# Index lists loaded per round into a doubled buffer, and comparisons on one row of 640, in a two-layer graph network

## What is computed

```python
# layer 0
h = x @ W
e = leaky_relu((h @ att_src)[src] + (h @ att_dst)[dst], 0.2)   # loops (i, i) added to the edges
e = exp(e - segment_max(e, dst)[dst])
alpha = e / (segment_sum(e, dst)[dst] + 1e-16)
x = layernorm(x + tanh(segment_sum(h[src] * alpha[:, None], dst) + bias))
# layer 1
h = gelu(x @ W_pre + b_pre)
x2 = x + segment_sum(h[src] * edge_attr, dst)
y = gelu(gelu(x2 @ W1 + b1) @ W2 + b2)
out = layernorm(x + x2 + y)
```

## Time and profile before

| | |
|---|---|
| median of 3 runs | 3725.67 us (3724.6 to 3725.97) |
| span of the profiled execution | 3722.8 us |
| busy: PE, DVE, ACT, POOL | 2393.6, 2438.3, 1283.2, 2781.1 us |
| gathers L690 | 2850, 946 ns each |
| PE's granted clock | 0.50 in most of layer 0, about 0.94 in layer 1 |

### The profile page before, as it was taken

The page is one execution under the profiler, slowest core; times in us unless marked ns, Lnnn a source line. Parts: engine busy times, 40 slices in busy tenths (PEclk is TensorE's granted clock), DMA queues, the critical chain, the costliest instruction groups (busy, mean ns, idle before and its releaser), DMA issues.

```text
span 3722.8 us, 66966 instructions
## 1 busy us (share of the span) xinstructions
PE 2393.6 (64%) x16704; PEld 1951.7 (52%) x16705; DVE 2438.3 (65%) x6240; ACT 1283.2 (34%) x3893; POOL 2781.1 (75%) x2950
## 2 busy tenths in 40 slices
PE   6433343434344444444445988989888989999888
PEld 3333333333333333333334777777776777777776
DVE  7444444444466666566666777777777788888886
ACT  5433343434445555555553111111111221111222
POOL 7777777777777777777775777777777777777776
PEclk7555555555555555555557999999999999999998
DMA  5222221222222222222223343443334343444332
GB/s 102 43 42 42 41 44 42 44 42 43 42 43 44 43 44 43 43 44 45 44 45 99 93 94 90 95 94 94 95 91 96 93 96 91 97 95 99 93 95 70
DMA packets 351632, 254.26 MB, mean 68 GB/s; under 512 B 254125, under 2 KB 279218, under 8 KB 351387
## 3 DMA queue, kind: packets, MB, share of 16 engines
q0 software_dynamic: 94016, 146.16, 17.8%
q1 hardware_dynamic: 242753, 99.71, 11.7%
q10 hardware_dynamic: 14618, 6.14, 0.6%
HBM read 244.43 MB, written 7.25 MB: 68 GB/s over the span
## 4 chain that ended last, share of the span: by engine, by line
POOL 60%; issue 24%; ACT 4%; DVE 4%; PE 3%; DMA 2%; ACTq 1%; DVEq 1%; POOLq 0%; SPq 0%
POOL rows L690 60%; ACT onehot L747 1%; DMA rows<-table,src_i 1%; DMA src_i<-in_src_dram 1%; PE bank L1086 1%; ACT L790 1%; ACTq L740 0%; ACT pair L767 0%; DVE score L1361 0%; PE bank L1029 0%; PE bank L962 0%; ACT rowu L796 0%; DVE bst L1399 0%; ACT unused L790 0%; DVE newp L1352 0%
## 5 line engine op out<-in xcount | busy, mean ns | idle before, releaser
L690 POOL DMA_INDIRECT rows<-table,src_i x2850 | 2694.8, 946 | 896.0 <-issue 859.5
L1086 PE MATMUL bank<-node,hot 128*128 128x288 bf16 x9310 | 1228.4, 294 | 28.1 <-issue 16.5
L995 PE MATMUL bank<-onehot,rows 128*97 128x72 f32 (+1 forms) x3048 | 584.9, 369 | 814.9 <-ACT onehot L777 814.9
L1086 PEld LDWEIGHTS bank<-node,hot 128*128 128x128 bf16 x9310 | 932.2, 101 | 282.4 <-issue 20.9
L995 PEld LDWEIGHTS bank<-onehot,rows 128*97 128x97 f32 x3048 | 530.8, 281 | 854.4 <-issue 792.5
L1505 DVE TENSOR_SCALAR hot<-node,key 128x642 bf16<-128x642 int16 x1862 | 870.3, 539 | 130.8 <-PE bank L1086 80.0
L900 ACT ACTIVATE pair<-dst_i 128x8 f32<-128x8 int32 x196 | 35.2, 180 | 1175.3 <-DVE rows L1531 904.3
L747 ACT ACTIVATE onehot<-iota,far_dst 128x72 f32 (+1 forms) x1564 | 384.4, 328 | 23.0
L1339 DVE SCALAR_TENSOR_TENSOR other<-onehot,bank 128x576 f32<-128x576 f32 (+1 forms) x196 | 121.9, 622 | 404.1 <-ACT bank L760 335.4
L1073 PE MATMUL bank<-onehot,rows 128*96 128x40 f32 (+1 forms) x3128 | 306.8, 256 | 88.4 <-DVE rows L1536 50.6
L1073 PEld LDWEIGHTS bank<-onehot,rows 128*96 128x96 f32 x3128 | 295.8, 170 | 110.1 <-issue 88.7
(11 more groups left out here) (204 smaller groups left out, 1931.1 us busy)
## 6 DMA issues: line engine op xcount, KB each, us to landing
attr<-in_edge_attr_dram SPq DMA_DIRECT2D x190, 336.0 KB
rows<-table,src_i POOLq DMA_INDIRECT x2850
node<-in_src_dram SPq DMA_DIRECT2D x195, 64.0 KB
attr<-in_edge_attr_dram SPq DMA_DIRECT2D x190, 48.0 KB
dst_i<-in_dst_dram SPq DMA_DIRECT2D x200, 4.0 KB
src_i<-in_src_dram SPq DMA_DIRECT2D x195, 4.0 KB
src_i<-in_src_dram SPq DMA_DIRECT2D x190, 3.5 KB
dst_i<-in_dst_dram SPq DMA_DIRECT2D x190, 3.5 KB
```

Source lines behind the costliest of these rows:

```text
L690: pool.indirect_dma_start(rows[:, u, j * width:(j + 1) * width], None, table, bass.IndirectOffsetOnAxis(ap=src_i[:, u, j:j + 1], axis=0))\
L995: last = pe.matmul(total[:, 0:w], rows0(u, it)[:, j, 0:D1], wide(weights, w)[:, j, :], start=j == 0, stop=j == most - 1)
L1086: last = pe.matmul(p_got[t], hot[:, c % HOTS, i, t * P:(t + 1) * P], tab[:, a, :, :].rearrange("p k d -> p (k d)"), start=a == 0, stop=a = ...
```

## The change

Index lists: `src_i` and `dst_i` get a leading dimension of 2, `src_next` goes. SP loads a whole round's lists with one transfer each into the half that the round does not use (`round_of`, `load_round1`), so a round's five groups share `e.src[0]` and `e.dst[0]`. In layer 0 it does that when the round before the running one is fully released; in layer 1 after the `attr` loads of slot 4 of each round. POOL waits once a round for the list and, from round 2 of layer 0 and round 1 of layer 1 on, at each slot for `free >= 5 it + u + 1` itself. `rounds` writes two rounds in a loop's body. `load_booked_src` becomes one transfer. ACT and DVE find the round's half of `dst_i` by a computed address (`dst_here`). The last group's lists are loaded one group earlier.

Comparisons: `src16` is one row of 640, `hot` is written as one row of 640 (of 642 in memory).

```diff
-        src_i = sb("src_i", [P, SLOTS, TILES], INT32)
+        src_i = sb("src_i", [P, 2, SLOTS, TILES], INT32)
-        src_next = sb("src_next", [P, SLOTS, TILES], INT32)
-        dst_i = sb("dst_i", [P, SLOTS, TILES], INT32)
+        dst_i = sb("dst_i", [P, 2, SLOTS, TILES], INT32)
...
-        src16 = node[:, at_src16:at_got].bitcast(INT16).rearrange("p (r e) -> p r e", r=3)
+        src16 = node[:, at_src16:at_got].bitcast(INT16)[:, 0:BOOKED * P]
...
+        def rounds(eng, body, alone):
+            for it in range(alone):
+                body(it, it % 2)
+            with eng.Fori(alone // 2, (ROUNDS - 1) // 2) as pair:
+                for k in range(2):
+                    body(pair * 2 + k, k)
+            body(ROUNDS - 1, (ROUNDS - 1) % 2)
...
+            def round_of(to, of, it, k, landed, ahead=0):
+                sp.dma_start(to[:, k, :, :], of_round(of, it, ahead).rearrange("u (p j) -> p u j", j=TILES))\
+                    .then_inc(landed, 16)
...
+            def load0(it, k):
+                if not first(it):
+                    sp.wait_ge(e0.free, (it + 1) * SLOTS)
+                if it is ROUNDS - 1:
+                    return
+                if first(it):
+                    sp.wait_ge(e0.dst[0], 16)
+                round_of(dst_i, dst, it, 1 - k, e0.dst[0], 1)
+                if not first(it):
+                    round_of(src_i, src, it, 1 - k, e0.src[0], 1)
...
+            def load1(it, k):
+                for u in range(SLOTS):
+                    load_attr(it * SLOTS + u, it, u)
+                    if u == 0 and not first(it):
+                        load_booked_src(it)
...
+                if it is not ROUNDS - 1:
+                    load_round1(it, k)
...
-                    pool.wait_ge(e.src[u], 16 * (it + 1))
-                    pool.sem_inc(g_go, 1)
...
+            def gather1(it, k):
+                pool.wait_ge(e1.src[0], 16 * (it + 1))
+                pool.sem_inc(g_go, 1)
+                for u in range(SLOTS):
+                    if not first(it):
+                        pool.wait_ge(e1.free, it * SLOTS + u + 1)
+                        pool.sem_inc(g_go, 1)
+                    for j in range(TILES - booked(it, u)):
+                        row_gather(rows[:, u, j * D:(j + 1) * D], table1, src_i[:, k, u, j:j + 1], e1.rows[u])
...
-                act.activation(src16[:, :, 0:ROW3], src_all.rearrange("p (r e) -> p r e", r=3), ACT.Copy)\
-                    .then_inc(g_src16, 1)
+                act.activation(src16, src_all[:, 0:BOOKED * P], ACT.Copy).then_inc(g_src16, 1)
...
-                    last = v.tensor_scalar(hot[:, c % HOTS, i, :].rearrange("p (r e) -> p r e", r=3),
-                                           src16[:, :, 0:ROW3], key[:, a:a + 1], None, ALU.is_equal)
+                    last = v.tensor_scalar(hot[:, c % HOTS, i, 0:BOOKED * P], src16, key[:, a:a + 1], None, ALU.is_equal)
```

More of the change, by code:

```diff
@@ L523, in _ @@
             sp.dma_start(x1[0:LAST_N, (CHUNKS - 1) * CB, 0:D], x[(CHUNKS - 1) * CN:N, :]).then_inc(s_x[-1], 16)
[L524 to L530, removed]
+            round_of(dst_i, dst, 0, 0, e0.dst[0])
+            sp.wait_ge(e0.src[0], 16)
+            round_of(src_i, src, 1, 1, e0.src[0])
             sp.dma_start(w_prex[0:D, :], w_pre).then_inc(s_w, 16)
@@ L550, in store_table @@
                 sp.dma_start(table0[(CHUNKS - 1) * CN:N, :], x1[0:LAST_N, (CHUNKS - 1) * CB, :]).then_inc(a_st, 16)
[L552 to L564, removed]
-                    sp.dma_start(dst_i[0:m, u, 0:t], dst[bass.ds(g * GE, n)].rearrange("(p j) -> p j", j=t))\
-                        .then_inc(e.dst[u], 16)
-                    if attrs:
-                        sp.dma_start(attr[0:m, u, 0:t * D],
-                                     edge_attr[bass.ds(g * GE, n), :].rearrange("(p j) d -> p (j d)", j=t))\
-                            .then_inc(e.attr[u], 16)
-                return body
@@ L637, in _ @@
             store_table()
[L638 removed]
+            rounds(sp, load0, alone=2)
+            load_last(e0)
             sp.wait_ge(e0.free, GROUPS + SLOTS)
[L640 removed]
+            round_of(src_i, src, 0, 0, e1.src[0])
+            round_of(dst_i, dst, 0, 0, e1.dst[0])
+            rounds(sp, load1, alone=2)
+            sp.wait_ge(e1.free, LAST + 1)
+            load_last(e1)
+            sp.dma_start(attr[0:LAST_E // LAST_T, 0, 0:LAST_T * D],
+                         edge_attr[LAST * GE:E, :].rearrange("(p j) d -> p (j d)", j=LAST_T)).then_inc(e1.attr[0], 16)
             sp.wait_ge(f_o, MCHUNKS + 1)
@@ new lines, in gather_last, with gather0 @@
+            def gather_last(e, free, table, width):
+                pool.wait_ge(s_last, 16)
+                pool.wait_ge(free, LAST + 1)
+                for j in range(LAST_T):
+                    row_gather(rows[:, 0, j * width:(j + 1) * width], table, src_last[:, j:j + 1], e.rows[0])
+            def gather0(it, k):
+                for u in range(SLOTS):
+                    if first(it):
+                        pool.wait_ge(e0.src[u], 16)
+                        for j in range(TILES):
+                            row_gather(rows0(u, it)[:, j, 0:D], x, src_i[:, 0, u, j:j + 1], e0.rows[u])
+                        continue
+                    if u == 0:
+                        pool.wait_ge(e0.src[0], 16 * (it + 1))
+                        pool.sem_inc(g_go, 1)
+                    if second(it):
+                        if u == 0:
@@ L689, in body @@
-                    for j in range(TILES - (e is e1 and booked(it, u))):
-                        pool.indirect_dma_start(rows[:, u, j * width:(j + 1) * width], None, table,
-                                                bass.IndirectOffsetOnAxis(ap=src_i[:, u, j:j + 1], axis=0))\
-                            .then_inc(e.rows[u], 16)
-                return body
-            groups(pool, gather(e0, table0, D2), alone=2)
+                        pool.wait_ge(e0.rows[u], 16 * TILES)
+                    else:
+                        pool.wait_ge(e0.free, it * SLOTS + u + 1)
+                        pool.sem_inc(g_go, 1)
@@ L696, in _ @@
+            rounds(pool, gather0, alone=2)
+            gather_last(e0, e0.free, table0, D2)
             pool.wait_ge(m_st, STORED)
-            groups(pool, gather(e1, table1, D), alone=1)
+            rounds(pool, gather1, alone=2)
+            gather_last(e1, e1.free, table1, D)
         @block.scalar
```

128 lines of the change are left out of this document (65 added, 63 removed).

## The result

The changed kernel takes 3736.88 us, median of 8 runs (3734.95 to 3738.14), against 3725.84 for the kernel before (8 runs, 3724.44 to 3728.23). The ratio is 1.0029 [1.0020, 1.0038], 11.0 us slower. The forecast was 22 us slower. The direction was right, and so was the rule for what a single gather loses. The one term that carried the forecast is half of what was expected, because gathers don't come at any phase to the comparisons.

The account below looks back on a forecast made before the run. POOL, issuing gathers without a break, was taken to bound the kernel. Span 3722.8 + 0 for loads, addresses and DVE's saving + 22 for held gathers = 3744.8; the runs' median is 2.9 above that span, so 3748; range 3724 to 3790.

Parts of the forecast that it names:

- The loads, gain 0: Index loads per round and POOL's own slot wait: POOL has no wait for a load to win, so 0.
- Computed addresses off POOL's path, 0: ACT's and DVE's computed addresses for dst lie off POOL's path and cost 0.
- The comparison at 370 ns: Layer 1's comparison on one row of 640 runs at a quarter of the plain rate, 370 ns against 539.
- DVE's saving is worth 0: Faster comparisons take 313 us of DVE work off layer 1, worth 0 because DVE is not last there.
- A gather loses T - 0.125 - x above an onset: A gather starting x after a DVE operation of length T loses this, for x above an onset of 0.075.
- Gathers come every 1.249 us, at any phase: Averaging the loss over all phases in layer 1: 0.0116 us per comparison, times 1862 = 22 us.
- rival B: A gather needs the shared way twice, for its indices and its writing: twice 22, 3770; chance 0.12.
- A: One-row comparison keeps its pace, two a step, and leaves gathers alone: 3726; chance 0.13.
- C: Comparison keeps its 0.539 but holds gathers back as the copy L1423 does: 86 us, 3811; chance 0.05.
- E: The round's index list lands late, at 20 us costing 230: 3956; chance 0.02.
- F: New order frees POOL's wait at slot starts, at the full gap 390 x 0.30 = 117 faster: 3609; chance 0.03.
- D: DVE doesn't let POOL in between two comparisons of a run: 400 us, 4126; chance 0.04.

Follow-up runs that it names:

- the kernel with the larger operation: Changed kernel with an unused reduction over 2 x 80 numbers before each comparison: 3753.86 us, ratio 1.0080.
- The widths 752 and 512: Changed kernel with each comparison 752 numbers wide, 3758.76 us; with each 512 wide, the fifth slot's comparisons left out, 3732.95 us.
- two experiments: Changed kernel with comparisons reading 32-bit numbers, 3871.23 us; changed kernel with an unused reduction of 2 x 16 numbers before each comparison, 3787.45 us.

## Why the prediction was right and wrong, step by step

**What bounds the kernel: right.** POOL issues without a break, and the time followed the gathers' lengths.

**The loads, gain 0: right.** With them alone the kernel is at 1.0005 [0.9996, 1.0014], and POOL has no wait for `src_i` behind the first.

**Computed addresses off POOL's path, 0: slightly wrong.** ACT's first operation of each group waits longer, beginning with the kernel before (busy, mean ns, idle before), then the changed one:

```profile
L744 ACT ACTIVATE far_dst<-dst_i 128x8 f32<-128x8 int32 x196 | 40.8, 208 | 147.0 <-issue 147.0
```

```profile
L793 ACT ACTIVATE far_dst<-dst_i 128x8 f32 (+1 forms) x196 | 40.8, 208 | 168.0 <-issue 147.4 <-DMA dst_i<-in_dst_dram 20.7
```

21 us more over 196 groups, 0.107 each. Between the layers POOL waits for layer 0's last groups, which are worked off one after the other; the distance of two of these went from 7.46 to 7.52 us in the median, and POOL's wait from 27.7 to 28.7. In the kernel with the loads alone the same group shows 168.1 and the wait 28.6; with the comparisons alone they are 147.3 and 27.7. So the 1.0 us belongs to the half of the change with the loads and the addresses.

Which of the two it is can be seen within one trace. ACT computes the address only in the groups of its loops; in the rounds that are written out the address is a constant, while the list comes in one piece in both. Nothing else in ACT's part of layer 0 was changed but the semaphore that it waits for. The timelines of ACT, the kernel before and then the changed one (a shape of `dst_i` is printed only where the address is a constant):

```profile
919.69 0.21 ACT L744 ACTIVATE far_dst<-dst_i 128x8 f32<-128x8 int32 x1 [0.84 <-issue]
929.14 0.21 ACT L744 ACTIVATE far_dst<-dst_i 128x8 f32<-128x8 int32 x1 [0.69 <-issue]
```

```profile
919.48 0.21 ACT L793 ACTIVATE far_dst<-dst_i 128x8 f32 x1 [0.93 <-issue]
929.27 0.21 ACT L793 ACTIVATE far_dst<-dst_i 128x8 f32<-128x8 int32 x1 [0.69 <-issue]
```

In the 175 groups with a computed address the idle time is 0.120 us longer than before, in the 21 with a constant one 0.001 (with the loads alone 0.120 and 0.007). So the computed address makes the 21 us; the 20.7 that the page puts down to the load of `dst_i` are the idle times of 23 groups in which that load was the last event, and most of each is there before the change too. That POOL's 1.0 us comes from these 0.12 a group was argued from the distances, not tested by itself.

**The comparison at 370 ns: right.** The source view of the changed kernel, ns min/median/max:

```profile
L1554 DVE TENSOR_SCALAR hot<-node,key x1862: 366/379/629, 2011.4 to 3681.0; 128x640 bf16<-128x640 int16 x187
```

Undisturbed it takes 366. The mean of 399 contains what gathers take from it, which is why DVE saved 251 us and not 313. The table of modes of the Trainium skill ("VectorE: DVE Perf Modes", § The perf-mode tier table) gives four numbers a step for this form; the trace agrees, since 512, 640 and 752 numbers take 332, 366 and 395 ns at least, 0.26 ns a number, a quarter of the 1.05 of the earlier trace rows.

**DVE's saving is worth 0: right**, and the kernel with the larger operation shows the other end of it.

**A gather loses T - 0.125 - x above an onset: right for a gather's start.** An x of 0.10 costs 0.156, 0.15 costs 0.106; the onset lies at 0.085, where I had taken 0.075 (at 0.08 to 0.10 some pay and some don't). It is not the whole cost of such operations: the second access above has no term in the sum, and in this kernel it needs none.

**"Gathers come every 1.249 us, at any phase": this step failed.** It turned the rule into 0.0116 us for each of 1862 comparisons. Length and onset aren't to blame: with the measured 0.38 and 0.085 in the same formula T - 0.125 - a stays 0.170, and the sum stays 22. Spread evenly, 1862 x 0.02/1.249 = 30 gathers would start in each 0.02 us behind a comparison's start. There are at most 17 from 0.08 to 0.22, and 355 from 0.22 to 0.24, where the loss is 0.007. The term of 22 us measures 10.1 by single gathers and 11.45 by the stretch. The hint stood in the rows that I had used against rival B: the scaling's own lengths of 310 to 552 show DVE held by gathers in mid-gather. I asked whether this costs POOL a second time, and didn't ask where it puts DVE's next operation. Today's three-row comparisons, which nothing holds, are indeed at any phase (the kernel with the loads alone), and I had carried this over to comparisons that are held. The widths 752 and 512 moved the locked phase to 0.20 to 0.22 (gathers lose 31.0 us) and to 0 and 0.27 (4.7 us): the lock is shown by these, not argued.

**The rivals.** A, C and E didn't come. F, a faster start of the slot, didn't either: the gap is 0.30 at any gather. B and D were given chances of 0.12 and 0.04 and don't show in this kernel, but two experiments show that what they were made of is real: a gather needs the shared way a second time, and it can then get it only at the end of a comparison, sometimes of the last of the run. I had discarded D on one gather that got on between two operations; it got in at its start, and the second access is another matter.

The SBUF page of the Trainium skill ("SBUF — State Buffer", § Who interferes with whom) says that a two-port operation of DVE and one of GpSimd exclude each other for the whole instruction. For DVE's operations the trace agrees in the main: a gather that starts more than 0.085 after one waits until 0.125 before its end. For the gather it doesn't: comparisons start and run at full pace beside most of its 0.94 us (0.37 at 2060.25, 0.28 into a gather). Those that start 0.50 to 0.70 after it are held as a rule (medians of 0.45 to 0.56), many of those at 0.70 to 0.80 too (0.39 and 0.45), and the others take 0.37 to 0.39.

## What to carry to other kernels

A faster mode of one engine can be paid by its neighbour: before you speed up an engine that isn't last, look in the trace for what the new form does to the one that is. When two engines hold each other in turn, don't average over the phase; work out where each one's hold puts the other's next start, and follow it through two or three periods. A cost that sits at the edge of such a phase is fragile: 0.03 us more length changed the gathers' loss in comparisons from 10 us to 31, and a spacing 0.09 us wider changed it to 63, of which the moved phase makes 27. And two engines can meet in more than one place of an operation: look at what a long one ends with, not only at what it starts in.

## What the runs showed of the hardware that was not expected

- A gather of 0.94 us holds fast comparisons in its middle, until about 0.73 after its start: of those that begin 0.50 to 0.70 after it, 340, the median takes 0.45 to 0.56, and the longest of all, 0.629, began 0.47 after one. In the kernel with the loads alone the comparisons in three rows are held nowhere (0.525 to 0.552 all over the 1.25 us between two gathers) and hold nobody.
- A gather needs a second access, and waits for it until a comparison ends; the gather's own end comes 0.12 us later. With comparisons of 0.54 that start 0.463 apart this cost 375 gathers 0.16 each. A gather can also be shut out over a whole run: 2.47 to 3.65 us with those comparisons, 1.81 to 2.21 us with comparisons of 0.37 that start 0.389 apart. With comparisons of 0.37 that start 0.297 apart no gather that met them took over 1.192. What decides whether a gather gets in after one comparison or only after the run isn't settled.
- An operation that holds nobody, put between those that do, made the kernel 50 us slower than the changed kernel when it was small and 17 us when it had five times as many numbers, the latter for another reason.
